# Gated rows exchanged between partition groups: one hop from SBUF to SBUF in sixteen transfers, in place of two hops through a buffer in DRAM

## The reference, cut to what matters

```
x = x + mixing(ctx, ctx, layernorm(x))            # 16 x 512 rows of 1024
xs = layernorm(x) as 8192 rows
tkw, top8 = route(xs @ router_w)                  # 8 of 32 experts for a row
h  = silu(xs_e @ w_gate[e]) * (xs_e @ w_up[e])    # 1024 -> 512, rows of expert e
routed = sum over 8 experts of (h @ w_down[e]) * tkw
shared = silu(xs @ sw_gate) * (xs @ sw_up) @ sw_down   # 1024 -> 1024 -> 1024
x = x + routed + shared
```

## Time and profile before

| What | us |
|---|---|
| Median of three runs | 13451.88 |
| The profiled execution's own time | 13453.46 |
| Its span, first to last instruction | 13451.6 |
| TensorE busy in the span (98%) | 13130.2 |
| VectorE busy (43%) | 5799.6 |
| ScalarE busy (23%) | 3144.8 |
| GpSimd busy (46%) | 6166.7 |

### The profile page before, as it was taken

The page is one execution under the profiler, slowest core; times in us unless marked ns, Lnnn a source line. Parts: engine busy times, 40 slices in busy tenths (PEclk is TensorE's granted clock), DMA queues, the critical chain, the costliest instruction groups (busy, mean ns, idle before and its releaser), DMA issues.

```text
span 13451.6 us, 191958 instructions
## 1 busy us (share of the span) xinstructions
PE 13130.2 (98%) x59424; PEld 10911.5 (81%) x59425; DVE 5799.6 (43%) x6536; ACT 3144.8 (23%) x4072; POOL 6166.7 (46%) x6373
## 2 busy tenths in 40 slices
PE   8999998999999999999999999999998999999999
PEld 7888887888888888787888887877787888888887
DVE  6888886333333333333334333334334333333333
ACT  4444442111122122212112121222222112111111
POOL 5588884101444444444444444444444444444111
PEclk9999999999999999999999999999999999999999
DMA  3344444554445454545445444555545444444444
GB/s 122 118 121 121 117 116 132 127 132 136 98 114 116 96 116 114 140 104 127 103 109 148 100 108 117 133 127 142 143 115 160 98 96 116 96 97 104 127 129 120
DMA packets 901031, 1597.84 MB, mean 119 GB/s; under 512 B 169521, under 2 KB 550705, under 8 KB 874738
## 3 DMA queue, kind: packets, MB, share of 16 engines
q0 software_dynamic: 246272, 609.25, 22.5%
q1 hardware_dynamic: 170738, 633.63, 15.0%
q10 hardware_dynamic: 483840, 352.54, 10.2%
HBM read 995.41 MB, written 599.86 MB: 119 GB/s over the span
## 4 chain that ended last, share of the span: by engine, by line
PE 77%; DMA 2%; DVE 2%; issue 1%; ACT 1%; ACTq 0%; DVEq 0%; SPq 0%
PE gps L1323 26%; PE ups L1323 26%; PE yps L1323 25%; DMA hsd<-hb 1%; DVE wlo L1238 1%; DMA hz<-hsd 1%; DMA raw<-in_w_gu_dram 0%; DVE xlo L1238 0%; ACT xhi L1156 0%; DVEq L961 0%; ACT whi L1150 0%; ACTq L1162 0%; DVE hp L1274 0%; DVE hb L1276 0%; ACTq L961 0%
## 5 line engine op out<-in xcount | busy, mean ns | idle before, releaser
L1108 POOL DMA_INDIRECT x2d<-yrow,yidx x544 | 945.2, 1738 | 3838.9 <-issue 1532.9
L1073 POOL DMA_INDIRECT xg<-xnd,xidx x2176 | 2156.8, 991 | 970.8 <-POOL xidx L1069 472.1
L1238 DVE TENSOR_TENSOR xlo<-xt,xhi 128x1024 fp32r<-128x1024 f32 x672 | 822.3, 1224 | 3851.3 <-ACT xhi L1156 3851.3
L1323 PE MATMUL gps<-whi,xhi 128*128 128x512 f32 x5376 | 2099.1, 390 | 106.5 <-DVE wlo L1238 88.1
L1323 PE MATMUL gps<-wlo,xhi 128*128 128x512 f32 x5376 | 2094.6, 390 | 0.0
L1323 PE MATMUL ups<-whi,xhi 128*128 128x512 f32 x5376 | 2094.5, 390 | 0.0
L1323 PE MATMUL gps<-whi,xlo 128*128 128x512 f32 x5376 | 2094.5, 390 | 0.0
L1323 PE MATMUL ups<-wlo,xhi 128*128 128x512 f32 x5376 | 2094.1, 390 | 0.0
L1323 PE MATMUL ups<-whi,xlo 128*128 128x512 f32 x5376 | 2093.6, 389 | 0.0
L1323 PE MATMUL yps<-whi,hhi 128*128 128x512 f32 x5376 | 1668.2, 392 | 130.4 <-DVE wlo L1238 122.5
L1323 PE MATMUL yps<-wlo,hhi 128*128 128x512 f32 x5376 | 1662.5, 391 | 0.0
(11 more groups left out here) (188 smaller groups left out, 17203.5 us busy)
## 6 DMA issues: line engine op xcount, KB each, us to landing
hsd<-hb ACTq DMA_DIRECT2D x2688, 64.0 KB
hz<-hsd ACTq DMA_DIRECT2D x672, 256.0 KB, 2.7
raw<-in_w_gu_dram SPq DMA_DIRECT2D x136, 1024.0 KB, 7.0
raw<-in_w_dn_dram SPq DMA_DIRECT2D x68, 1024.0 KB, 6.8
yrow<-x2d SPq DMA_DIRECT2D x128, 512.0 KB, 3.6
kT<-in_ctx_dram SPq DMA_DIRECT2D x64, 704.0 KB, 8.8
xg<-xnd,xidx POOLq DMA_INDIRECT x2176
xin<-in_x_dram SPq DMA_DIRECT2D x64, 512.0 KB
```

The source lines that it names most:

```text
L1073: pool.indirect_dma_start(out=xg[i][:, q, :], out_offset=None, in_=quarters, in_offset=bass.IndirectOffsetOnAxis(ap=xidx[i][:, q:q + 1], a ...
L1108: pool.indirect_dma_start(out=acc, in_=yrow[i][:, :], in_offset=None, out_offset=bass.IndirectOffsetOnAxis(ap=yidx[i][:, 0:1], axis=0), co ...
L1238: return dve.tensor_tensor(dst, src, hi.bitcast(F32), ALU.subtract)
L1323: ins = pe.matmul(ps, rows, w[:, chunk, i * 512:(i + 1) * 512], start=first and n == 0, stop=last_one and n == 2)
```

## The change

`spread_h` now moves each of the sixteen blocks of 32 partitions by 128 numbers (16 KB) from `hb` straight to its place in `hz`, SBUF to SBUF. `collect_h`, the buffer `hsd` and the semaphore `h_st` are gone. The sixteen transfers are issued where the four were, ahead of `yrow`; all raise `h_ld`, 256 for a tile. The wait for `h_lo`, which protects `hz` of the tile before, moves from the read to the spread; silu's wait, which protects `hb`, is now for `h_ld` of the tile before.

```diff
-            def spread_h(t, slot):
+            def spread_h(t):
                 act.wait_ge(h_turned, t + 1)
+                wait(act, h_lo, t)
                 for q in range(QUADS):
-                    act.dma_start(hsd[slot].rearrange("(b r) q x -> r b q x", r=SQ)[:, :, q, :],
-                                  hb[q * SQ:(q + 1) * SQ, :].rearrange("r (b x) -> r b x", x=P)).then_inc(h_st, 16)
-
-            def collect_h(t, slot):
-                act.wait_ge(h_st, 16 * QUADS * (t + 1))
-                wait(act, h_lo, t)
-                act.dma_start(hz[:, :, :, :].rearrange("p q k s -> p (q k s)"),
-                              hsd[slot].rearrange("p q x -> p (q x)")).then_inc(h_ld, 16)
+                    for a in range(QUADS):
+                        act.dma_start(hz[a * SQ:(a + 1) * SQ, q, :, :].rearrange("r k s -> r (k s)"),
+                                      hb[q * SQ:(q + 1) * SQ, a * P:(a + 1) * P]).then_inc(h_ld, 16)
...
-                    wait(act, h_st, 16 * QUADS * t)
+                    wait(act, h_ld, 16 * QUADS * QUADS * t)
                     act.activation(hb[:, :], gps[:, :], ACT.Silu).then_inc(silu_done, 1)
...
-                    spread_h(t, c.slot())
+                    spread_h(t)
...
-                    collect_h(t, c.slot())
-                    act.wait_ge(h_ld, 16 * (t + 1))
+                    act.wait_ge(h_ld, 16 * QUADS * QUADS * (t + 1))
```

More of the change, by code:

```diff
@@ L890, in feed_forward @@
     xnd, acc, lists, out = A["xnd"], A["x2d"], A["lists"], A["out"]
-    hsd = A["hsd"]
     quarters = xnd.rearrange("n (a l) -> (n a) l", a=QUADS)
@@ L948, in feed_forward @@
         gu_mm, down_mm = sem("gu_mm"), sem("down_mm")
-        x_turned, h_turned, h_st, h_ld = sem("x_turned"), sem("h_turned"), sem("h_st"), sem("h_ld")
+        x_turned, h_turned, h_ld = sem("x_turned"), sem("h_turned"), sem("h_ld")
         silu_done, h_done = sem("silu_done"), sem("h_done")
@@ L1373, in program @@
     A["lists"] = nc.dram_tensor("lists", (E * LIST, 2), I32).ap()
-    A["hsd"] = nc.dram_tensor("hsd", (2, P, QUADS, P), F32).ap()
     A["tabd"] = nc.dram_tensor("tabd", (TCOLS * P * FIELDS,), I32).ap()
```

## The result

The changed kernel takes 14153.85 us (14135.77 to 14164.88, four runs) against 13450.06 (13446.27 to 13455.85, four runs): the ratio is 1.0522, with a 95% interval of 1.0503 to 1.0540. It is slower by 704 us. The profiled execution took 14161.52 us, its span is 14159.6. I had forecast 13442 with a range up to 13500, so the measured time lies 654 us outside the range, and even my slower rival gave 13498.

A forecast was written before the change was run, and what follows sets the result against it. TensorE was taken as the bound, busy 13130.2 of 13451.6 us, so the exchange could change only its waits. Terms +8 + 4 + 1 - 18 - 3 - 2 = -10 us gave 13442 us from the median; range 13408 to 13500.

The forecast's parts named there:

- my slower rival: Spread on ScalarE's queue: each issue costs 0.48 us whatever its pieces; +46 us, 13498 us; chance 0.22.
- Issue: Spread on ScalarE's queue: sixteen issues at 0.34 us each, the last issued at 5.4 us; 7.7 with 0.48 throughout.
- Landing: End of the spread: SBUF to SBUF landing between 1.35 and 2.62 us, 2.0 taken for first tiles; one landing replaces two.
- The cover: Ordinary tiles: exchange 1 to 1.5 us later against 5.2 us before TensorE waits; no cost, even at 10.3 us.
- The sixteen and the three: Experts' first tiles without slack for the low down weights: exchange 7.4 us against 6.9 and 5.96; +8 and +4 us.
- the seven that I had costed at nothing: Seven first tiles where `hlo` stands behind the gate and up split on VectorE and `hhi` has microseconds to spare; cost nothing.
- The last tile: Layer's last tile, nothing to hide behind: exchange 7.0 us against 5.8, TensorE waiting for `hlo`; +1 us.
- The tile after a first tile: Two loads run beside its exchange: issues cheapen once loads end, `hhi` at about 10 us, short waits go; -2 us.
- The seven under load: Seven first tiles with six 1 MB loads beside the exchange: fewer hops save 2.6 us each; -18 us.
- rival C: Tiles under load: smaller transfers get fewer queue turns, gain only 0.3 us each; +11 us, 13463 us; chance 0.15.
- The order on ScalarE: `yrow` behind the sixteen issues starts at 5.4 us, not 2.0, delaying GpSimd's scatter and gathers; cost 0.
- Rival A: Spread's issues: a price per transfer, not per piece, 0.48 us each, `hhi` at 9.7; +46 us, 13498 us; chance 0.22.

## Why the prediction was wrong, point by point

- **Issue: the step that failed.** I took 0.34 us an issue and 0.48 at most. It is 0.54 for the first and 0.64 from then on: the sixteenth ends at 10.14 us, not 5.4, and above my upper bound of 7.7. Two errors are in it. The first is the reading of 0.34 against 0.48 as a matter of the pieces a transfer has: sixteen writes of 32 pieces cost what four of 128 did. The first issue after a pause is cheaper, and those that follow it are dearer. The second is that I bounded the landing of an unseen SBUF to SBUF transfer from both sides, but not its issue, which I took from rows with one side in DRAM as if these were the same operation.
- **Landing.** I said 1.35 to 2.62, 2.0 taken. It is 1.4 in ordinary tiles and 1.6 at the sixteen first tiles, measured from the end of the last issue. There the term was right. It was not in the 19 tiles ahead of a first tile, where the longer exchange runs into the loads: 6.9 us.
- **The cover.** That an exchange up to 11.1 us is hidden in ordinary tiles was right: at 9.0 us 490 tiles lost 8 us, at 11.6 they lost 242. I had called even the upper bound, 10.3, hidden and so never asked what lies behind it. Just behind it nearly every tile pays, some 0.35 us, and this stage has 672. Nor did the sum have a term for the clock: down parts behind the long waits ran slower, 167 us in all.
- **The shared expert's tiles.** I gave them no line in the sum. Half of the 706 us is theirs (+345). Their landing is longer in the first half (3.6 us), their issues are in the second (12.2 us for sixteen).
- **The sixteen and the three.** I worked out +12 at 0.5 and 1.4 us each, and the sixteen alone lost 79: 5.0 us each with `hhi` 5.0 us later. One for one, as argued; the size came from the issues. The three lost 11, and the seven that I had costed at nothing 17. The last tile, +1 in the sum, waits 11.45 us for `hlo` where it was 3.91.
- **The tile after a first tile.** I took -2 and `hhi` at about 10 us, as issues would cost 0.34 again once the loads end. `hhi` came at 12.4, and these 24 tiles lost 37 us.
- **The seven under load.** I forecast -18, measured -25; first issue to `hhi` fell from 21.4 to 17.8. In one of them, TensorE's wait is now 11.91 us:

```profile
5961.52 1.22 PE L1317 MATMUL yps<-whi,hhi 128*128 128x512 f32 x2 [11.91 <-DVE wlo L1232]
```

  It was 15.79. By rival C this gain would not have come, only 0.3 in each. The exchange under load took 17.8, 17.4, 14.7 and 9.1 us with sixteen, twelve, eight and one transfers, so fewer help, but sixteen in one hop were already quicker than five in two. The Trainium skill (DMA: Bandwidth & Descriptors, "Queues, rings and completion order") has an engine drain a whole packet of descriptors from one queue before it turns to the next, by which C would hold; the gain speaks against that here, though no run isolates it.
- **The order on ScalarE.** I costed the later `yrow` at nothing. It starts 10.4 us after the first issue, not 5.4, and VectorE waits for the gathers in 521 tiles, before in 57, 3023 us against 278. No run shows that this cost TensorE anything: with twelve transfers the wait was 1986 us and the ordinary tiles lost 8. What I missed is that the later `yrow` was of use.
- **Rival A** had the mechanism of the result, a price for each transfer, and gave +46 us since it took 0.48 as the highest price. At 0.64 the same sum crosses the cover, which A never reached.
- The Trainium skill (DMA: Bandwidth & Descriptors, "Issuing engines are not separate DMA queues") calls the time to initiate a transfer usually small beside the transfer. Here it was 0.64 against a landing of 1.4, and sixteen times over it is most of the exchange. The same page's advice under "Rules for kernel authors", to coalesce many small transfers into one, agrees with the eight and the one.

## What to carry to other kernels

Count the issues of a queue that computes or waits in between, and price each from a transfer with the same kinds of memory on both sides; where none is in the trace, the bound has to reach well above the rows at hand. Compare the lengthened chain with its cover for every kind of tile, and put the range's end where the cover is passed, as the loss there is multiplied by the number of tiles. Where blocks only change partition groups, copies by an engine with time to spare need no queue at all.

## What the runs showed of the hardware that I had not expected

- The price of an issue on ScalarE's queue: 0.31 and in a row 0.44 us with one side in SBUF, 0.51 and 0.61 with both, for 16 and 64 KB to DRAM, and for 16 and 32 KB within SBUF, alike. A single one of 256 KB took 0.35 from DRAM and 0.48 within SBUF. Why two sides in SBUF cost more was not settled.
- ScalarE and VectorE can write a block of 32 partitions to another group of 32; 32 by 128 numbers take 0.31 us on either. Sixteen such operations cost eight times one of the full width for a copy (0.63) and seven times for a transpose (0.72).
- GpSimd's scatter and gathers beside the last small transfers lengthened their landing from 1.4 to 3.5 us, and the kernel's time from 1.0535 to 1.1349 of before. Four loads of 1 MB beside them made it 6.9 us.
- Behind a wait of 5.07 us TensorE ran at a granted clock of 0.50 for some 4 us, then at 1.00.
